# Two layers of attention and FFN on one core: late statistics and output weights split around the first iteration, chunk 7's contexts divided first at chunk 8, last sums closed and normalised one by one

## The chip, the cores and the metric

One core of one Trainium2 chip. The metric is the device time of one execution in microseconds, lower is better. The kernel is a single launch on this core. TensorE is PE in the rows, VectorE is DVE, ScalarE is ACT, GpSimd is POOL, and SyncE's queue is SPq.

## The reference

An array x of 1024 tokens by 512 passes through four steps. Each adds the result of a block to x and normalises the sum over the 512 columns:

```
x = layernorm(x + attn0(x))   # 32 heads of 16; per TOKEN a softmax of q k^T over the heads
x = layernorm(x + ffn0(x))    # three +1/-1 weight matrices, relu between
x = layernorm(x + attn1(x))   # rotary, causal window of 128, 32 query heads and 8 key heads, output weights Wo
x = layernorm(x + moe(x))     # shared experts + the best 2 of 16 experts per token, weighed
```

with `layernorm(x) = (x - mean) / sqrt(var + 1e-5)`. The first attention is unusual: for each token a 32 x 32 matrix of scores between heads, softmax, times the 32 values.

## The kernel before, in words

The tokens are eight tiles of 128 rows (T = 8), kept as X[128, tile, 512] in two groups of four (G = 4). Each engine has its own program, written out by hand in the order in which it is to run; they wait for each other through semaphores. PSUM banks are used in rings: `fill` is PE's wait until a bank is free, `take` the reader's wait until it is full, and `drained` the wait until it has been read.

*First attention.* 16 chunks k, eight for each group, each with the scores of 16 token columns for the four tiles. For a chunk PE makes scores(k + 2), a projection of the other group, and values(k). DVE runs `shift(k + 1)` (maximum and difference, L1010 and L938), `turn_weights(k)` (L1019), and `contexts(k - 1)` (L1025 and L938), which divides the weighted values of the chunk before by their sum. ACT takes the exponentials. At k = NCH = 8 the first group is complete: PE turns its contexts (`contexts(0, ...)`, L424, four banks through a ring of two), which waits for DVE's contexts(7), and DVE adds them to X (`add_contexts`, four additions). Around this POOL and SP issue the small transfers that lay values and keys out for the chunks, and ACT issues loads of later weights.

*Normalisation.* In three steps: DVE's `stats` (L965 and L966: mean and variance of a tile), ACT's `roots` (square root, L1499, where every ACT operation is recorded), DVE's `rates` (L1068, L1069: reciprocal and offset), then ACT's `normalise` for each tile. The semaphores `stats_ready`, `std_ready` and `offset_ready` count batches; the batches are numbered.

*FFN, then second attention.* The second group's last FFN layer (`last_layer(1, j)`) runs inside the loop of the second attention. That loop goes over i = -1 to 7 in eight steps s. In iteration i PE makes the row scores of tile i + 1 (L582), for whose row maxima DVE runs `row_maxima` (L1205), and the key scores of tile i (L595), on which ACT takes exponentials, POOL sets the triangle to zero (L1860, L1863), and PE weighs the values (L610). Row maxima are brought as extra rows into the stack of queries (`turn_maxima`, `maxima_out`, L1219, and POOL's `stack_maxima`, L1852); key scores wait for them. The projections of tile i + 2 (L524), its rotation and its way through DRAM back into stacks (SP L881, POOL L1846) lie in the same iteration; the output of tile i - 1 too. In i = -1 there are no key scores yet. There DVE also sums the FFN result into X (`ffn_out`: L1056, then statistics), takes the rates of batch 4 at step 6, and ACT takes the roots and normalises tiles 4 to 7 at step 6. The output weights `ao` are loaded by SP (L839), copied by ACT (`high_part(15, ...)`, i = 0, step 6) and their rest is subtracted by POOL (L1877, i = 1, step 0).

*MoE and the tail.* Routing, then a list ITEMS of 39: four shared experts for group 0, one for group 1, 31 blocks of 128 routed rows, and the last three shared experts of group 1. For each item PE makes `up(k)`, ACT the silu, DVE the product (for a shared expert with a cast and a difference), and PE `down(k)`. The blocks' results go to DRAM and are gathered again by POOL. For tiles 0 to 3 DVE adds the gathered rows (`combine`). For tiles 4 to 7 PE adds them to the accumulators, through diagonal matrices (`add_routed(t)`, L807), and closes them with the last shared expert (`down`, L761), one flag `sum_closed` for each tile. DVE adds each to X (`collect`), then takes statistics and rates (`last_stats`, batches 7, 8 and 9 for tiles 0 to 3, 4 and 5, 6 and 7), ACT normalises and SP stores (L923).

Of the kernel before, what the change touches and what calls it, by code (L numbers as in the profile page):

```python
# [11 lines left out]
ALU = mybir.AluOpType  # L12
# [6 lines left out]
T = 1024 // P  # L19
G = 4  # L20
# [14 lines left out]
NCH = P // CH  # L35
# [44 lines left out]
def build(nc, x, wq, wk, wv, bias, k0, k1, k2, s0, s1, s2, aq, ak, av, ao, gate, experts, shared,  # L80
          rope_c, factor_c, table_c, out, xs, ys):
    with ExitStack() as ctx:
# [256 lines left out]
        def _(pe):  # L339
# [410 lines left out]
            def down(k):  # L750
                if ITEMS[k][0] == "shared":
# [6 lines left out]
                    for j in range(G):  # L758
                        closed = e == SE - 1
                        for n, (l, r) in enumerate(((hi, dh), (hi, dl), (lo, dh))):  # L760
                            mm = nc.tensor.matmul(acc[j][:, :], l[:, j * P:(j + 1) * P], r,  # L761
                                                  start=(e == 0 and n == 0), stop=(closed and n == 2))
                        if g == 1 and closed:
                            mm.then_inc(sum_closed, 1)
# [45 lines left out]
            for t in range(G, T):  # L810
                add_routed(t)
            down(len(ITEMS) - 1)


# [113 lines left out]
        def _(v):  # L928
# [122 lines left out]
            def ffn_out(g, *which):  # L1051
                ring = (V, A)[g]
                for j in which:
                    t = g * G + j
                    b = ring.take(v, ("ffn", t))
                    nc.vector.scalar_tensor_tensor(X[:, t, :], b[:, :], scales[:, 2:3], X[:, t, :], ALU.mult, ALU.add)\  # L1056
                        .then_inc(ring.free, 1)
                    ring.drained(v, ("ffn", t))
                    ins = stats(t)
                    if j < G - 1 and t > 0:  # L1060
                        ins.then_inc(dve, 1)
                        steps[0] += 1
                    else:
                        ins.then_inc(stats_ready, 1)

# [37 lines left out]
            for k in range(2 * NCH):  # L1103
                if k + 1 < 2 * NCH:
                    shift(k + 1)
# [9 lines left out]
                if k >= 1:  # L1115
                    contexts(k - 1)
# [152 lines left out]
            for i in range(-1, T):  # L1269
                t, r, d = i + 2, i + 1, i - 1  # L1270
                for s in range(8):
# [23 lines left out]
                    if i == -1 and s in (2, 4, 5, 6):  # L1295
                        ffn_out(1, (2, 4, 5, 6).index(s))
                    if s == 5 and r < T:
                        maxima_out(r, 0)
                    if (i, s) == (-1, 6):
                        rates(slice(G, T), 4)  # L1300
# [121 lines left out]
            def last_stats(tiles, batch):  # L1422
# [7 lines left out]
                v.wait_ge(std_ready, batch + 1)  # L1430
                q = slice(tiles[0], tiles[-1] + 1)
                own(nc.vector.reciprocal(rstd[:, q], std[:, q]))
                nc.vector.scalar_tensor_tensor(offset[:, q], mv[:, q, 0], -1.0, rstd[:, q], ALU.mult, ALU.mult).then_inc(offset_ready, 1)

            nshared = 0
            for k, item in enumerate(ITEMS):
# [42 lines left out]
                if k == len(ITEMS) - 2:  # L1479
# [4 lines left out]
                    last_stats(range(0, G), 7)  # L1484

            for a in range(G, T, 2):
                for t in (a, a + 1):
                    v.wait_ge(sum_closed, t - G + 1)
                    collect([t], [banks[4 + t - G]])
                v.wait_ge(x_summed, a + 2)  # L1490
                last_stats(range(a, a + 2), 8 + (a - G) // 2)
# [3 lines left out]
        def _(s):  # L1495
# [190 lines left out]
            for i in range(-1, T):  # L1686
                t, d = i + 2, i - 1
                for step in range(8):
# [15 lines left out]
                    if (i, step) == (-1, 6):  # L1704
                        roots(slice(G, T), 4)
                        s.wait_ge(offset_ready, 5)
                        for t4 in range(G, T):
                            normalise(t4)
                    if (i, step) == (0, 6):
                        high_part(15, 3, raw_c[3], wc_in[3])  # L1710
# [55 lines left out]
            for n, (a, b) in enumerate(((0, G), (G, G + 2), (G + 2, T))):  # L1766
# [7 lines left out]
        def _(p):  # L1774
# [97 lines left out]
            for i in range(-1, T):  # L1872
                t, r = i + 2, i + 1
                for step in range(8):
                    if (i, step) == (1, 0):
# [86 lines left out]
```

## Time and profile before

| | |
|---|---|
| median of 3 runs | 686.64 us (685.29 to 689.45) |
| profiled execution, its own time | 688.42 us |
| its span, first to last instruction | 686.7 us |
| mean granted TensorE clock | 0.952 |
| busy: PE, DVE, ACT, POOL | 596.6, 398.3, 271.0, 221.8 us |
| share of the span | 87%, 58%, 39%, 32% |
| transfers | 99.41 MB, mean 145 GB/s |

The busy time counts an engine's instructions while they run; a matmul's end is modelled. The profile's span is shorter than the time of its execution by what lies around the first and the last instruction. The granted clock is the share of full speed that TensorE was given. In a timeline row the number in brackets is the idle time of that engine before the instruction, and behind the arrow stands what ended it; "issue" is no visible wait, "remote" one whose releaser the profile doesn't tell.

### The profile page before, as it was taken

How to read it: one execution, taken by the hardware profiler on the slowest of the kernel's cores; microseconds unless marked ns; L12 is line 12 of the kernel's file. 1: busy time of each engine (PE TensorE's matmuls, PEld its weight loads, DVE VectorE, ACT ScalarE, POOL GpSimd, SP SyncE). 2: the span in 40 equal slices, each digit the busy share in tenths (PEclk: the TensorE clock that was granted, in tenths of full speed). 3: DMA queues.
4: the chain of work that ended last, by engine and by line, in shares of the span. 5: the costliest groups of instructions: out<-in, count | busy, mean ns of one | idle time of the engine just before them, and what ended most of it. 6: DMA issues, size and time to landing. Idle time of an engine off the chain costs nothing.

```text
span 686.7 us, 13474 instructions
## 1 busy us (share of the span) xinstructions
PE 596.6 (87%) x5125; PEld 470.7 (69%) x5125; DVE 398.3 (58%) x1142; ACT 271.0 (39%) x433; POOL 221.8 (32%) x313
## 2 busy tenths in 40 slices
PE   2998999767898977999999997978799999999894
PEld 1987986656677655776777766755477788788672
DVE  3414643797775767878778787622676243232265
ACT  5155118347744334344353444536410223222205
POOL 5001434264500015544464445451002132231270
PEclk9999999989999988899999999766999999999998
DMA  9100110262134626153361426022115499999373
GB/s 307 68 0 20 48 45 20 63 196 88 40 84 153 215 62 216 42 178 101 118 212 54 171 98 224 4 88 79 50 40 187 156 358 389 389 415 367 118 194 131
DMA packets 45680, 99.41 MB, mean 145 GB/s; under 512 B 11760, under 2 KB 18032, under 8 KB 43440
## 3 DMA queue, kind: packets, MB, share of 16 engines
q1 hardware_dynamic: 27280, 56.70, 22.9%
q0 software_dynamic: 12720, 31.61, 14.6%
q10 hardware_dynamic: 5616, 10.23, 4.1%
q8 instruction: 42, 0.69, 0.4%
q14 instruction: 22, 0.18, 0.1%
HBM read 67.96 MB, written 25.95 MB: 137 GB/s over the span
## 4 chain that ended last, share of the span: by engine, by line
PE 57%; DVE 14%; ACT 11%; DMA 9%; issue 5%; POOL 1%; SPq 1%; ACTq 0%; DVEq 0%
PE bank L343 15%; PE bank L524 11%; PE bank L379 9%; DMA slots_out<-FP 6%; DVE FP L938 5%; ACT FP L1499 4%; PE bank L610 4%; PE bank L595 3%; PE bank L582 3%; PE bank L761 2%; DVE kraw L1205 2%; PE bank L390 2%; ACT W L1499 1%; ACT XR L1499 1%; ACT X L1499 1%
## 5 line engine op out<-in xcount | busy, mean ns | idle before, releaser
L1499 ACT ACTIVATE FP<-bank 128x512 f32<-128x512 f32 (+1 forms) x244 | 138.7, 611 | 289.8 <-PE bank L595 98.8
L1205 DVE CUSTOM_DVE_ANT_0 kraw<-bank,maskb 128x256 bf16<-128x256 f32 (+1 forms) x256 | 88.4, 400 | 33.0 <-PE bank L582 33.0
L524 PE MATMUL bank<-W,XR 128*128 128x512 f32 x348 | 100.6, 432 | 1.6 <-DVE XR L938 1.5
L343 PE MATMUL bank<-FP 128*128 128x128 f32 x558 | 89.0, 312 | 2.4 <-ACT FP L1499 2.4
L379 PE MATMUL bank<-W,XR 128*128 128x512 f32 x288 | 76.2, 414 | 5.2 <-DVE W L938 5.2
L524 PEld LDWEIGHTS bank<-W,XR 128*128 128x128 f32 x348 | 67.0, 204 | 16.4 <-DVE XR L938 2.0
L379 PEld LDWEIGHTS bank<-W,XR 128*128 128x128 f32 x288 | 63.6, 271 | 11.1 <-DVE W L938 5.6
L1894 POOL DMA_INDIRECT FP<-slots_in,index x31 | 29.8, 963 | 125.8 <-PE bank L726 65.8
L1860 POOL TENSOR_SCALAR_AFFINE_SELECT FP<-FP 128x512 f32<-128x512 f32 x64 | 39.7, 644 | 91.6 <-ACT FP L1499 91.6
L343 PEld LDWEIGHTS bank<-FP 128*128 128x128 f32 x558 | 65.6, 192 | 4.9 <-issue 2.9
L938 DVE TENSOR_TENSOR FP<-FP,bank 128x128 f32<-128x128 f32 (+1 forms) x39 | 14.4, 369 | 64.8 <-ACT FP L1499 48.8
L343 PE MATMUL bank<-RP,W 128*128 128x512 f32 x192 | 45.8, 394 | 3.5 <-DVE FP L938 3.5
L1863 POOL TENSOR_SCALAR_AFFINE_SELECT FP<-FP 128x512 f32<-128x512 f32 x56 | 38.9, 719 | 24.2 <-ACT FP L1499 24.2
L343 PEld LDWEIGHTS bank<-RP,W 128*128 128x128 f32 x192 | 35.7, 188 | 12.0 <-issue 1.9
L1820 POOL DMA_DIRECT2D RPF<-FP x64 | 31.7, 502 | 34.8 <-PE bank L415 23.3
L1444 DVE COPY FP<-bank 128x512 f32<-128x512 f32 x31 | 21.4, 691 | 30.0 <-PE bank L726 30.0
L938 DVE TENSOR_TENSOR XR<-bank,XR 128x512 fp32r<-128x512 f32 x27 | 21.3, 805 | 30.2 <-ACT XR L1499 30.2
L610 PE MATMUL bank<-FP 128*17 128x128 f32 x960 | 36.8, 302 | 1.8 <-ACT FP L1499 1.6
L610 PEld LDWEIGHTS bank<-FP 128*17 128x17 f32 x960 | 26.1, 106 | 12.5 <-issue 5.8
L582 PE MATMUL bank<-RP,QS 64*128 64x256 f32 x160 | 21.9, 353 | 11.2 <-DVE hmax L1205 9.6
L595 PE MATMUL bank<-QS,RP 64*128 64x128 f32 x320 | 26.1, 285 | 4.3 <-ACT FP L1499 2.3
L595 PEld LDWEIGHTS bank<-QS,RP 64*128 64x128 f32 x320 | 23.8, 207 | 7.1 <-ACT FP L1499 3.0
(179 smaller groups left out, 960.5 us busy)
## 6 DMA issues: line engine op xcount, KB each, us to landing
FP<-in_experts_dram SPq DMA_DIRECT2D x31, 768.0 KB
slots_out<-QS SPq DMA_DIRECT2D x48, 256.0 KB, 3.0
RP<-slots_out POOLq DMA_DIRECT2D x8, 1024.0 KB, 5.3
slots_out<-FP ACTq DMA_DIRECT2D x31, 256.0 KB
QS<-slots_out POOLq DMA_DIRECT2D x5, 1024.0 KB, 6.8
XR<-slots_out POOLq DMA_DIRECT2D x3, 1024.0 KB, 6.0
FP<-in_shared_dram SPq DMA_DIRECT2D x4, 768.0 KB, 4.3
RPF<-FP POOLq DMA_DIRECT2D x64, 34.0 KB, 2.0
```

Source lines behind the costliest of these rows:

```text
L343: mm = nc.tensor.matmul(bank, lhs, rhs, start=(n == 0), stop=(n == len(terms) - 1))
L379: mm = nc.tensor.matmul(b[:, :], *terms[m], start=(m == 0), stop=(m == 3 * DC - 1))
L524: mm = nc.tensor.matmul(b[:, :], *terms[n], start=(n == 0), stop=(n == len(terms) - 1))
L582: mm = nc.tensor.matmul(both[a][:, m, :], qS[i % 3][half(a, KS), pr, :], kS[half(a, KS), slots, pr, :], start=True, stop=True)
L595: mm = nc.tensor.matmul(both[a][:, m * P:(m + 1) * P], kS[half(a, KS), (i - w) % 4, pr, :], qS[i % 3][half(a, KS), pr, :], start=True, sto ...
L610: mm = nc.tensor.matmul(weighing[32 * q:32 * q + HD + 1, (h // 4 % 4) * P:(h // 4 % 4 + 1) * P], vaug[:, (i - w) % 4, head(h), :], PT[hg % ...
L938: return nc.vector.tensor_tensor(o, a, b, op)
L1205: ins = nc.vector.tensor_tensor_reduce(masked[:, 2 * (f % 2) + m, 0:n], b[:, m, :], maskb[:, m0:m0 + n], 1.0, -BIG, ALU.add, ALU.max, hmax ...
L1499: return nc.scalar.activation(o, i, func, **kw)
L1820: nc.gpsimd.dma_start(vdiag[k % 3][32 * g:32 * g + 32, 272 * g:272 * g + 272].rearrange("p (s d) -> p s d", s=CH), vT[32 * g:32 * g + 32, ...
L1860: ins = nc.gpsimd.affine_select(out=pt, in_=pt, compare_op=ALU.is_ge, fill=0.0, base=0, pattern=[[0, 4], [1, P]], channel_multiplier=-1)
L1863: ins = nc.gpsimd.affine_select(out=pt, in_=pt, compare_op=ALU.is_ge, fill=0.0, base=-1, pattern=[[0, 4], [-1, P]], channel_multiplier=1)
```

## The change

Three parts.

1. At chunk 8 DVE runs contexts(7) ahead of shift(9) and turn_weights(8) instead of behind them.
2. `ffn_out` is cut into `ffn_sum` and `ffn_stats`. In i = -1 the second group's sums stay where they were; all four statistics go to i = 0, step 0, the rates and the roots to i = 0, step 1, and ACT's four normalisations to step 5. ACT's copy of the output weights goes from i = 0, step 6, to i = -1, step 6, and POOL's subtraction from i = 1, step 0, to i = -1, step 7.
3. In the tail `last_stats` no longer takes the rates, so that DVE doesn't wait for the root of tiles 0 to 3 ahead of the last activation. PE adds the routed rows of tiles 4 to 6, closes their sums, and then adds and closes tile 7. DVE takes sums and statistics in turn with the rates; tiles 6 and 7 are normalised as batches of their own.

```diff
@@ tensor
-            def down(k):
+            def down(k, *which):
...
-                    for j in range(G):
+                    for j in which or range(G):
...
-            for t in range(G, T):
+            for t in range(G, T - 1):
                 add_routed(t)
-            down(len(ITEMS) - 1)
+            down(len(ITEMS) - 1, *range(G - 1))
+            add_routed(T - 1)
+            down(len(ITEMS) - 1, G - 1)
@@ vector
+            def ffn_sum(g, j):
+                ring = (V, A)[g]
+                t = g * G + j
+                b = ring.take(v, ("ffn", t))
+                nc.vector.scalar_tensor_tensor(X[:, t, :], b[:, :], scales[:, 2:3], X[:, t, :], ALU.mult, ALU.add)\
+                    .then_inc(ring.free, 1)
+
+            def ffn_stats(g, *which):
...
+            def ffn_out(g, *which):
+                for j in which:
+                    ffn_sum(g, j)
+                    ffn_stats(g, j)
...
             for k in range(2 * NCH):
+                if k == NCH:
+                    contexts(k - 1)
                 if k + 1 < 2 * NCH:
                     shift(k + 1)
...
-                if k >= 1:
+                if k >= 1 and k != NCH:
                     contexts(k - 1)
...
                     if i == -1 and s in (2, 4, 5, 6):
-                        ffn_out(1, (2, 4, 5, 6).index(s))
+                        ffn_sum(1, (2, 4, 5, 6).index(s))
+                    if (i, s) == (0, 0):
+                        ffn_stats(1, *range(G))
...
-                    if (i, s) == (-1, 6):
+                    if (i, s) == (0, 1):
                         rates(slice(G, T), 4)
...
-            def last_stats(tiles, batch):
+            def last_stats(*tiles):
...
                 ins.then_inc(stats_ready, 1)
-                v.wait_ge(std_ready, batch + 1)
-                q = slice(tiles[0], tiles[-1] + 1)
-                own(nc.vector.reciprocal(rstd[:, q], std[:, q]))
-                nc.vector.scalar_tensor_tensor(offset[:, q], mv[:, q, 0], -1.0, rstd[:, q], ALU.mult, ALU.mult).then_inc(offset_ready, 1)
+
+            def last_sum(t):
+
+                v.wait_ge(sum_closed, t - G + 1)
+                collect([t], [banks[4 + t - G]])
...
-                    last_stats(range(0, G), 7)
-
-            for a in range(G, T, 2):
-                for t in (a, a + 1):
-                    v.wait_ge(sum_closed, t - G + 1)
-                    collect([t], [banks[4 + t - G]])
-                v.wait_ge(x_summed, a + 2)
-                last_stats(range(a, a + 2), 8 + (a - G) // 2)
+                    last_stats(*range(0, G))
+
+            rates(slice(0, G), 7)
+            last_sum(G)
+            last_sum(G + 1)
+            v.wait_ge(x_summed, G + 2)
+            last_stats(G, G + 1)
+            last_sum(G + 2)
+            rates(slice(G, G + 2), 8)
+            v.wait_ge(x_summed, G + 3)
+            last_stats(G + 2)
+            last_sum(T - 1)
+            rates(slice(G + 2, G + 3), 9)
+            v.wait_ge(x_summed, T)
+            last_stats(T - 1)
+            rates(slice(T - 1, T), 10)
@@ scalar
                     if (i, step) == (-1, 6):
+                        high_part(15, 3, raw_c[3], wc_in[3])
+                    if (i, step) == (0, 1):
                         roots(slice(G, T), 4)
+                    if (i, step) == (0, 5):
                         s.wait_ge(offset_ready, 5)
                         for t4 in range(G, T):
                             normalise(t4)
-                    if (i, step) == (0, 6):
-                        high_part(15, 3, raw_c[3], wc_in[3])
...
-            for n, (a, b) in enumerate(((0, G), (G, G + 2), (G + 2, T))):
+            for n, (a, b) in enumerate(((0, G), (G, G + 2), (G + 2, T - 1), (T - 1, T))):
                 roots(slice(a, b), 7 + n)
@@ gpsimd
-                    if (i, step) == (1, 0):
+                    if (i, step) == (-1, 7):
                         p.wait_ge(w_high, 16)
                         nc.gpsimd.tensor_tensor(W[:, 7, :], raw_c[3], W[:, 6, :].bitcast(F32), ALU.subtract).then_inc(wo_split, 1)
```

## Rows read from the trace of the kernel before

**Rows 1.** Timeline of chunk 8, all engines: start, us, engine, line, operation, count, idle time.
```profile
133.48 0.68 DVE L1010 TENSOR_REDUCE small<-bank 128x16 f32<-128x512 f32 x1
...
135.43 0.22 DVE L1025 RECIPROCAL small<-bank 128x16 f32<-128x16 f32 x1
...
136.16 3.79 PE L424 MATMUL bank<-ident,FP 128*128 128x128 f32 x16 [3.22 <-DVE FP L938]
137.39 1.47 DVE L938 TENSOR_TENSOR X<-X,bank 128x512 f32<-128x512 f32 x2 [1.28 <-PE bank L424]
...
139.28 1.39 DVE L938 TENSOR_TENSOR X<-X,bank 128x512 f32<-128x512 f32 x2 [0.43 <-PE bank L424]
```

**Rows 2.** Windows, 136 to 140 us: busy time by engine, then clock, DMA share, GB/s.
```profile
136.00:140.00 4.00, 3.84 (x24) 3.20 (x28) 2.18 (x5) 1.44 (x1) 3.91 (x9) 0.57 0.86 262
```

**Rows 3.** Timeline of PE from i = -1 to i = 0.
```profile
244.26 0.44 PE L582 MATMUL bank<-RP,XR 64*128 64x128 f32 x4 [1.50 <-DVE hmax L1205]
247.44 0.80 PE L582 MATMUL bank<-RP,QS 64*128 64x256 f32 x4 [2.75 <-DVE hmax L1205]
...
248.92 4.58 PE L524 MATMUL bank<-W,XR 128*128 128x512 f32 x12
```

**Rows 4.** Timeline of DVE from i = -1 to i = 0.
```profile
243.20 0.27 DVE L1205 CUSTOM_DVE_ANT_0 kraw<-bank,maskb 128x128 bf16<-128x128 f32 x1
...
244.81 0.69 DVE L965 BATCH_NORM_STATS2 st<-X 128x6 f32<-128x512 f32 x1
...
246.08 0.18 DVE L1068 RECIPROCAL rstd<-std 128x4 f32<-128x4 f32 x1 [0.36 <-ACT std L1499]
...
253.96 0.42 DVE L1205 CUSTOM_DVE_ANT_0 kraw<-bank,maskb 128x256 bf16<-128x256 f32 x1 [4.25 <-PE bank L582]
```

**Rows 5.** Timeline of DVE in the tail.
```profile
671.88 0.18 DVE L1432 RECIPROCAL rstd<-std 128x4 f32<-128x4 f32 x1 [4.42 <-ACT std L1499]
...
672.27 0.69 DVE L938 TENSOR_TENSOR FP<-FP,bank 128x512 f32<-128x512 f32 x1
...
675.19 1.37 DVE L938 TENSOR_TENSOR X<-X,bank 128x512 f32<-128x512 f32 x2 [1.05 <-PE bank L761]
```

**Rows 6.** Timeline of ACT in the tail.
```profile
669.64 0.60 ACT L1499 ACTIVATE FP<-bank 128x512 f32<-128x512 f32 x1 [16.19 <-remote]
...
682.71 1.52 ACT L1499 ACTIVATE X<-X,offset,rstd 128x512 f32<-128x512 f32 x2 [0.43 <-DVE offset L1433]
```

**Rows 7.** Timeline of PE in the tail.
```profile
668.22 6.11 PE L807 MATMUL bank<-FP 128*128 128x512 f32 x13 [0.51 <-issue]
674.20 3.00 PE L761 MATMUL bank<-W,XR 128*128 128x512 f32 x12
```

**Rows 8.** Timeline of POOL, then of SP's queue, around i = -1 and 0.
```profile
243.99 1.17 POOL L1852 DMA_DIRECT2D XR<-QS  x2 [8.44 <-DVE QS L1219]
...
272.55 4.54 POOL L1877 TENSOR_TENSOR W<-WF,W 128x2048 fp32r<-128x2048 f32 x1
...
240.74 0.40 SPq L839 DMA_DIRECT2D WF<-in_ao_dram  x1
```

**Rows 9.** Issues of transfers, 238 to 250 us: count, KB each, us to landing.
```profile
WF<-in_ao_dram SPq DMA_DIRECT2D x1, 1024.0 KB, 5.2
XR<-QS POOLq DMA_DIRECT2D x2, 8.0 KB, 2.0
```

**Rows 10.** Timeline of ACT in i = 0.
```profile
249.44 1.28 ACT L1499 ACT_TABLE_LOAD   x1
...
257.84 1.08 ACT L1499 ACTIVATE FP<-bank 128x512 f32<-128x512 f32 x2 [6.03 <-PE bank L595]
...
269.50 1.08 ACT L1499 ACTIVATE FP<-bank 128x512 f32<-128x512 f32 x2 [3.44 <-PE bank L595]
270.48 1.91 ACT L1499 ACTIVATE W<-WF 128x2048 fp32r<-128x2048 f32 x1
```

**Rows 11.** Chain of waits at the end of i = 0: start, us, what.
```profile
268.83 6.82 DMA QS<-slots_out
```

More of the change, by code:

```diff
@@ L1049, in hidden_low @@
                     tt(dst[:, 1, o, :], hf[g][:, o % 2, :], dst[:, 0, o, :].bitcast(F32), ALU.subtract).then_inc(h_ready, 1)
-            def ffn_out(g, *which):
+            def ffn_sum(g, j):
[5 more added lines that the diff above has]
+            def ffn_stats(g, *which):
                 ring = (V, A)[g]
@@ L1054, in ffn_out @@
                     t = g * G + j
-                    b = ring.take(v, ("ffn", t))
-                    nc.vector.scalar_tensor_tensor(X[:, t, :], b[:, :], scales[:, 2:3], X[:, t, :], ALU.mult, ALU.add)\
-                        .then_inc(ring.free, 1)
                     ring.drained(v, ("ffn", t))
```

## The prediction

> **What bounds the kernel now.** I read the page first, then the chain of waits in order of time, to see which engine ends each stage, and then the timelines of the engines at the three places that the change touches. TensorE (PE) holds most of the chain, so an edit pays only where PE, or whoever holds the chain at that moment, waits for the work that is moved. The three places lie one behind the other, and what one gives the next ones pass on: in between, the kernel is chains of waits in a fixed order and loads that start on flags.
>
> **Chunk 8.** VectorE (DVE) works off chunk 9's shift, chunk 8's turned weights and then chunk 7's contexts (reciprocal at 135.43); PE turns the contexts only from 136.16, after 3.22 us of idle time that the difference L938 ends [rows 1]. DVE then waits 1.28 us for the first turned bank and 0.43 us for the third; its four additions end at 140.67 [rows 1]. PE ran these transposes at a mean granted clock of 0.57 over 136 to 140 us [rows 2].
>
> **Around the first iteration (i = -1 and 0).** In i = -1 PE stands 1.50 us before row scores 7 and 2.75 us before the first of i = 0, both times for DVE's maxima [rows 3]. DVE has in between the sum and the statistics of the last FFN tile, a wait of 0.36 us for the root from ScalarE (ACT), and the rates [rows 4]. In i = 0 it is the reverse: PE goes from 248.92 through a product of twelve matmuls in 4.58 us, and DVE stands 4.25 us [rows 3, 4].
>
> **The tail.** DVE waits 4.42 us for the root of tiles 0 to 3 before it touches the last activation [rows 5]; the root stands behind the last silu on ACT, which begins only at 669.64 [rows 6]. PE meanwhile adds the routed rows (thirteen matmuls to 674.33) and then closes four sums [rows 7].
>
> **The change part by part: contexts at chunk 8.** Contexts(7) hold DVE for 0.67 us (135.43 to 136.1) and need nothing but chunk 7's values, which PE had finished before its idle time. Moved to 133.48 they end at 134.15, so that PE may start 2.0 us earlier. The shift and the turned weights (133.48 to 135.43, 1.95 us) follow and end at 136.1; DVE's first addition starts there, 1.28 us earlier. Banks 3 and 4 can be filled only after the first additions. PE's sixteen transposes took 3.79 us, mostly at the lower clock, 0.95 us a bank; at the full level about half. At the full level the additions end near 139.0 (1.7 us gained, both waits); at the lower level each of the last two banks adds up to half a microsecond and they end near 139.7 (1.0 us) [rows 1]. PE's idle time shrinks from 3.22 to about 1.2 us, which speaks for the higher level, yet behind the first two banks PE has little to do. I take 1.3 us. What is late in its place: the shift, by 0.67 us, and with it the exponential and ACT's first conversion of kernel weights. DVE waits for neither in this stretch. If it did, the edit would cost those 0.67 us: the lower bound is a loss of 0.67, the upper a gain of 1.7.
>
> **Statistics and rates out of i = -1.** The last statistics begin at 244.81 and the rates at 246.08, with a reciprocal and a product to 246.4: 1.6 us between the last FFN sum and maxima 7 that go. The statistics of the tile before stand ahead of maxima 6 (243.20), which could start 0.45 us earlier, when its scores are there [rows 4]. So the first row scores of i = 0 start 2.05 us earlier, at 245.4 [rows 3]. Who is late next? The key scores behind them need the first half's maxima: POOL issues those two transfers at 243.99 in 1.17 us [rows 8], and such a transfer lands after 2.0 us [rows 9], near 246.6 if the second starts at 244.6. The maxima leave DVE some 0.6 us earlier, so 246.0, when PE, at 245.4 plus its scores, wants them. That is nearly level and the 2.05 us stand; if the transfer decides, 0.6 us is left.
>
> Four statistics (3.45 us, each 0.69 + 0.17) now stand behind maxima 0 of i = 0. Those end at 249.71 today, so at 247.65; DVE is free at 251.1, 2.85 us before the 253.96 of now [rows 4]. They are hidden in the 4.25 us of idle time, and 2.85 is also the most this part can give. It is reached if PE's product of 4.58 us finds the higher clock, where twelve such matmuls take 3.0 [rows 3, 7]. The rates (0.34 us) go in front of maxima 2 of i = 0; I count 0.1 us for them, since DVE waits a little behind these maxima. I take 2.3 us; bounds 0.6 and 2.85.
>
> **Output weights, roots and normalisation.** The load of the output weights is issued at 240.74 [rows 8] and lands after 5.2 us [rows 9], at 245.9; ACT's copy of 1.91 us [rows 10], now ahead of i = 0, ends at 247.9. Today ACT begins its table load for Exp at 249.44; behind the copy it can begin earlier, and the first exponentials come at 249.2 instead of 250.7. Sqrt now lies between two Exp: two table loads of 1.28 us more, and a root of 0.3 to 0.4. ACT is through with the exponentials at 250.3, has the root behind the statistics (251.1) and its own load (251.6) at 252.0 and the second load at 253.3. The key scores of step 2, at which ACT now stands 6.03 us until 257.84 [rows 10], are due 2.05 to 2.85 us earlier, from 255.0. Hidden. The four normalisations go into step 5: the two of 1.52 us in [rows 6] make 3.0 for four, within the 3.44 us of idle time before 269.50 [rows 10]; their tiles are turned only in iteration 1. POOL's subtraction (4.54 us, today at 272.55 [rows 8]) moves behind the copy, to 247.9; the first mask is kept until 252.4, but the first weighing is some eight microseconds away. That the copy leaves step 6 gives nothing: the next iteration starts on a stack transfer of 6.82 us begun at 268.83 [rows 11], which moves only with the rotation ahead of it.
>
> Here a rule of the Trainium skill speaks against the change. The rows show the table load of 1.28 us begun at 249.44, and nothing but that load in front of the exponential. The page "ScalarE: Activation LUTs" (What ACT_TABLE_LOAD costs) counts about 2.66 us for a switch, since it adds a drain. By that figure, an estimate, the three loads up to step 2 would end some 4 us later than above, 2 us past the need, and the sum would be less by these 2.
>
> **The tail.** Without the wait, the last product, cast and difference (1.9 us, from 672.27 to PE's start at 674.20 [rows 5, 7]) follow the silu's end at 670.25: the activation is there at 672.2. A matmul of the additions costs 0.45 us, a tile 1.8; tiles 4 to 6 are in at 672.5. The first sum reaches DVE 1.0 us later (today 675.19 behind 674.20), at 673.5. From there: two sums 1.4, two statistics 1.7, third sum 0.7, rates 0.35, third statistics 0.85, fourth sum 0.7 (its bank closes near 677.1, as today, for PE's work is only reordered): 679.2. The rates of tile 6 wait for ACT, which normalises 4 and 5 until 679.1 and has the root at 679.4: 679.75; statistics of the last tile 680.6, root 681.0, rates 681.3, one normalisation 0.8: 682.1. Today the last ends at 682.71 + 1.52 = 684.23 [rows 6]. Gain 2.1 us; the store behind it stays. Bounds: 1.6, if the five added hand-overs cost 0.1 us more each, and 2.6, if the first banks close that much earlier. The late silu changes little here: if it came early, the additions would decide in both kernels.
>
> **Sum.** 1.3 + 2.3 + 2.1 = 5.7 us. The profiled execution took 688.42 us (span 686.7 and 1.7 around it), so 682.7 for such a one. It lay 1.8 us above the median of the three runs; against that, 686.64 - 5.7 = 680.9 us.
>
> **Rivals.** (a) Both PE stretches find the higher clock and the banks close early: 1.7 + 2.85 + 2.6 = 7.15, 679.5 us. For it: less idle time of PE. Against: in i = -1 PE still has little to do between 242 and 246. (b) Transfers take most of the first iteration's gain: 1.3 + 0.6 + 2.1 = 4.0, 682.6 us. For it: two arrivals near 246.0. (c) A table load costs ACT twice its 1.28 us when work stands on both sides; three of them make 3.8 us, so ACT is ready at 257.1, 2 us past the need: 5.7 - 2.0 = 3.7, 682.9 us. Against it: the row at 249.44. The page named above holds with this one. (d) Slower: ACT, in program order, stands at the copy until the output weights are there, and all exponentials of i = 0 stand behind it. From the landing to an ACT ready for step 2 are 1.9 + 1.3 + 1.1 + 1.3 + 0.4 + 1.3 = 7.3 us, so 253.2 against 255.0: 1.8 us of slack. Each microsecond beyond costs one; the sum turns negative when the weights land 7.5 us late, a load of 12.7 instead of 5.2 us. At 9 us late: 688 us. No other large load is under way then, so it is unlikely.
>
> **How the numbers follow.** Forecast 0.60, (a) 0.16, (b) 0.13, (c) 0.07, (d) 0.04. A measurement of this kernel can tell about 1% (6.9 us) from no change. The range takes in (a) to (c), both less 1.6 us below and plus 2.1 above, for the lower bound of chunk 8 and the 1.4 us by which the fastest run lay under its median: 677.9 to 685.0. Faster by over 1% means below 679.8: most of (a) and a fourth of the forecast, 0.30. Within 1%: 0.67. Slower: 0.03.
>
> **What would show it.** Right: PE's idle time before the transposes of the contexts near 1 us; no idle time above 2 us on PE around row scores 7 and 0; four statistics in DVE's 4.25 us; two more table loads inside ACT's idle time; the first closed sum 1.7 us ahead of today's, and one normalisation alone at the end. Wrong: row scores of i = 0 early but key scores waiting for a transfer; ACT's copy long in waiting; iteration 1 starting on a transfer that has not moved.

## The result, and the profile after

The changed kernel took 680.81 us (median of 16 runs, 676.62 to 686.01), the kernel before 685.88 us beside it (16 runs, 681.97 to 690.89): ratio 0.9927, 95% interval 0.9903 to 0.9951, so 5.0 us gained. Two later jobs, each with its own runs of the kernel before, gave 0.9914 (0.9879 to 0.9950) and 0.9899 (0.9848 to 0.9951). The profiled execution took 680.29 us, span 678.6, against 688.42 and 686.7. Its mean granted clock is 0.958, before 0.952.

Chunk 8, from the timeline of the changed kernel (columns as in [rows 1]):

```profile
133.41 0.25 DVE L1027 RECIPROCAL small<-bank 128x16 f32<-128x16 f32 x1
...
134.04 0.68 DVE L1012 TENSOR_REDUCE small<-bank 128x16 f32<-128x512 f32 x1
...
135.98 1.25 DVE L940 TENSOR_TENSOR X<-X,bank 128x512 f32<-128x512 f32 x2
137.81 0.69 DVE L940 TENSOR_TENSOR X<-X,bank 128x512 f32<-128x512 f32 x1 [0.57 <-PE bank L424]
138.66 0.69 DVE L940 TENSOR_TENSOR X<-X,bank 128x512 f32<-128x512 f32 x1 [0.17 <-PE bank L424]
139.26 0.68 DVE L1012 TENSOR_REDUCE small<-bank 128x16 f32<-128x512 f32 x1
```
```profile
134.17 1.17 PE L424 MATMUL bank<-ident,FP 128*128 128x128 f32 x8 [1.30 <-DVE FP L940]
136.69 1.93 PE L424 MATMUL bank<-ident,FP 128*128 128x128 f32 x8 [1.35 <-DVE X L940]
```

The contexts' reciprocal is ahead of the shift's reduction, and PE's idle time before the transposes is 1.30 us instead of 3.22 [rows 1]. The first eight transposes take 1.17 us, the last eight 1.93: the granted clock falls to 1.2 GHz at 136.9 us, in between.

Around the first iteration, PE, then DVE, then ACT (against [rows 3, 4, 10]):

```profile
244.37 0.44 PE L582 MATMUL bank<-RP,XR 64*128 64x128 f32 x4 [1.11 <-DVE hmax L1218]
245.90 0.65 PE L582 MATMUL bank<-RP,QS 64*128 64x256 f32 x4 [1.09 <-DVE hmax L1218]
246.40 1.11 PE L595 MATMUL bank<-XR,RP 64*128 64x128 f32 x8
247.45 5.49 PE L524 MATMUL bank<-W,XR 128*128 128x512 f32 x12
...
275.93 0.50 PE L582 MATMUL bank<-RP,QS 64*128 64x256 f32 x4 [2.71 <-DMA QS<-slots_out]
...
277.58 4.24 PE L524 MATMUL bank<-W,XR 128*128 128x512 f32 x12
```
```profile
247.90 0.69 DVE L967 BATCH_NORM_STATS2 st<-X 128x6 f32<-128x512 f32 x1
...
251.01 0.18 DVE L968 BATCH_NORM_AGGREGATE mv<-st 128x2 f32<-128x6 f32 x1
253.42 0.42 DVE L1218 CUSTOM_DVE_ANT_0 kraw<-bank,maskb 128x256 bf16<-128x256 f32 x1 [2.23 <-PE bank L582]
```
```profile
245.97 1.91 ACT L1523 ACTIVATE W<-WF 128x2048 fp32r<-128x2048 f32 x1 [10.43 <-DMA WF<-in_ao_dram]
247.90 1.28 ACT L1523 ACT_TABLE_LOAD   x1
249.19 1.09 ACT L1523 ACTIVATE FP<-bank 128x512 f32<-128x512 f32 x2
250.30 1.28 ACT L1523 ACT_TABLE_LOAD   x1
251.59 0.30 ACT L1523 ACTIVATE std<-mv,epst 128x4 f32<-128x4 f32 x1
251.91 1.28 ACT L1523 ACT_TABLE_LOAD   x1
257.31 1.09 ACT L1523 ACTIVATE FP<-bank 128x512 f32<-128x512 f32 x2 [4.12 <-PE bank L595]
```

PE's two waits are 1.11 and 1.09 us instead of 1.50 and 2.75. Key scores follow at 246.40 without a wait, so no transfer stands in their way. DVE has the four statistics where it stood idle. ACT has three table loads, nothing between a load and its user, and still 4.12 us of idle time. But PE's product takes 5.49 us, which was 4.58 [rows 3], and iteration 1 begins on a stack transfer at 275.93, where it began at 275.75 before. Counted from the first row scores of i = -1 (228.13, before 227.64) that is 47.8 us for 48.1: in this profile the 2.0 us are down to 0.3 there.

The tail, in the same order (against [rows 5 to 7]):

```profile
661.59 5.31 PE L807 MATMUL bank<-FP 128*128 128x512 f32 x12
666.34 2.65 PE L761 MATMUL bank<-W,XR 128*128 128x512 f32 x9
668.83 1.88 PE L807 MATMUL bank<-FP 128*128 128x512 f32 x4
670.14 1.26 PE L761 MATMUL bank<-W,XR 128*128 128x512 f32 x3
```
```profile
664.59 0.17 DVE L1079 RECIPROCAL rstd<-std 128x4 f32<-128x4 f32 x1
...
667.64 1.38 DVE L940 TENSOR_TENSOR X<-X,bank 128x512 f32<-128x512 f32 x2 [2.69 <-PE bank L761]
```
```profile
656.34 0.60 ACT L1523 ACTIVATE FP<-bank 128x512 f32<-128x512 f32 x1 [7.56 <-PE bank L343]
...
671.64 1.52 ACT L1523 ACTIVATE X<-X,offset,rstd 128x512 f32<-128x512 f32 x2 [0.55 <-DVE offset L1080]
...
675.30 0.81 ACT L1523 ACTIVATE X<-X,offset,rstd 128x512 f32<-128x512 f32 x1 [0.43 <-DVE offset L1080]
```

The rates of tiles 0 to 3 cost no wait, sums 4 to 6 close before the last tile is added, and one normalisation of 0.81 us ends it at 676.11. From the first addition to that end it is 14.53 us, where it was 17.98 (684.23 less the first of the sixteen additions, of which [rows 7] has the last thirteen):

```profile
666.25 1.45 PE L807 MATMUL bank<-FP 128*128 128x512 f32 x3
```

The last silu came at 656.34, after 7.56 us of idle time: the 16.19 us of [rows 6] are in none of the other profiles.

### The profile page after: what moved, and what is told of

It is laid out like the page before. It is cut to its first block, busy times and chain, and to the rows that moved or that the text cites. A ratio compares the mean times of both kernels' runs of the same rounds, so it can differ in the third digit from the quotient of the medians.

```text
span 678.6 us, 13479 instructions
## 1 busy us (share of the span) xinstructions
PE 595.0 (88%) x5125; PEld 469.4 (69%) x5125; DVE 397.3 (59%) x1144; ACT 274.0 (40%) x436; POOL 221.3 (33%) x313
## 4 chain that ended last, share of the span: by engine, by line
PE 62%; DVE 12%; ACT 10%; DMA 8%; issue 5%; POOL 1%; SPq 1%; DVEq 0%; ACTq 0%
PE bank L343 19%; PE bank L524 11%; PE bank L379 9%; DVE FP L940 5%; ACT FP L1523 4%; DMA slots_out<-FP 4%; PE bank L610 4%; PE bank L582 3%; PE bank L595 3%; PE bank L761 2%; PE bank L402 2%; PE bank L390 2%; PE bank L726 1%; DVE kraw L1218 1%; ACT XR L1523 1%
## 5 line engine op out<-in xcount | busy, mean ns | idle before, releaser
L940 DVE TENSOR_TENSOR FP<-FP,bank 128x128 f32<-128x128 f32 (+1 forms) x39 | 14.4, 369 | 63.3 <-ACT FP L1523 47.5
L343 PE MATMUL bank<-RP,W 128*128 128x512 f32 x192 | 45.8, 394 | 3.5 <-DVE FP L940 3.5
L1845 POOL DMA_DIRECT2D RPF<-FP x64 | 31.6, 501 | 34.1 <-PE bank L415 23.0
L582 PEld LDWEIGHTS bank<-RP,QS 64*128 64x128 f32 x160 | 13.1, 195 | 22.4 <-DVE hmax L1218 11.1
```

Of the source, the lines that this page charges most:

```text
L343: mm = nc.tensor.matmul(bank, lhs, rhs, start=(n == 0), stop=(n == len(terms) - 1))
L582: mm = nc.tensor.matmul(both[a][:, m, :], qS[i % 3][half(a, KS), pr, :], kS[half(a, KS), slots, pr, :], start=True, stop=True)
L940: return nc.vector.tensor_tensor(o, a, b, op)
L1845: nc.gpsimd.dma_start(vdiag[k % 3][32 * g:32 * g + 32, 272 * g:272 * g + 272].rearrange("p (s d) -> p s d", s=CH), vT[32 * g:32 * g + 32, ...
```

## The experiments

Twelve experiments: nine new kernels, and three times one that had run before. Each has 6 to 12 runs, against 23 or 35 runs of the kernel before in the same job, and one profile. The gains in microseconds are worked out from the ratio. The time says what all of a kernel did; beside it I read three stretches of each profile, since the middle, which no edit touches (from the row scores of i = 6 to the first addition of the tail), took anything from 241.8 us (the first profile of the change) to 249.1. In the second and third profile of the change it took 246.1 and 243.4, in the kernel before 246.5, so most of what made the first one's middle short was chance.

**Each part alone, and the whole again.** Chunk 8's order only:

```
+                if k == NCH:
+                    contexts(k - 1)
...
+                if k >= 1 and k != NCH:
```

> Only chunk 7's contexts go ahead at chunk 8. If the parts add up (theory A), the additions at chunk 8 end 1.3 us earlier and the time is 1.3 us (0.2%) under before. If PE's clock level or a transfer takes the gain back before the second attention starts (theory B), the additions end 1.3 us earlier all the same, the first row scores of i = -1 start within 0.5 us of before, and the time is before's within 1 us.

The statistics, roots, rates, normalisations and output weights only:

```
+                        ffn_sum(1, (2, 4, 5, 6).index(s))
+                    if (i, s) == (0, 0):
+                        ffn_stats(1, *range(G))
...
+                        high_part(15, 3, raw_c[3], wc_in[3])
```

> Only the statistics, rates, roots, normalisations and output weights move around the first iteration. Theory A: first row scores of i = 0 2 us earlier, row scores of i = 1 2.3 us earlier, time 2.3 us under before. Theory B: the first is 2 us earlier, but PE's product behind it takes 5 us or more at the lower clock and the stack transfer 7 us or more, so the row scores of i = 1 start at most 0.5 us earlier and the time is before's within 1 us.

The tail only, both PE's order and the sums one by one:

```
+            down(len(ITEMS) - 1, *range(G - 1))
+            add_routed(T - 1)
...
+            last_sum(G + 2)
+            rates(slice(G, G + 2), 8)
```

> Only the tail is changed. Theory A: from the first addition of routed rows to the last normalisation 2.1 us less than in before's profile (18.0 us), time 2.1 us under before. Theory B (the tail is nearly all of the change): 3 us or more less, and the time 3.5 to 5 us under before.

All three, unchanged:

> The changed kernel once more, for a second profile and as the measure of the other three. Both theories: 4 to 6 us under before. If the 4.8 us by which the stretch from the second iteration to the first addition was shorter in its first profile were chance, it is another number here; if it belongs to the change, 4 us or more again.

Measured, against a before of 688.92 us: chunk 8 ratio 0.9983 (0.9945 to 1.0020), -1.2 us; first iteration 0.9972 (0.9928 to 1.0016), -1.9 us; tail 0.9969 (0.9930 to 1.0008), -2.1 us; all three 0.9914 (0.9879 to 0.9950), -5.9 us. (The plain medians, 686.67, 686.46, 685.75 and 680.93 us, lie 2.3, 2.5, 3.2 and 8.0 us under it.) The parts add up to -5.2, and nothing speaks for a part that works only beside another, within intervals that are some 5 us wide. None of the three alone is told from zero by its interval; the profiles have to do that:

| stretch | profiles without the part | with it | gain |
|---|---|---|---|
| chunk 8: copy of its values to the shift of chunk 10 | 8.99 to 9.51 (7) | 8.25 to 8.29 (4) | 0.7 to 1.3 |
| the same copy to the first row scores | 96.55 to 97.57, mean 97.16 (7) | 96.25 to 97.11, mean 96.62 (4) | 0.5 |
| row scores of i = -1 to those of i = 0 | 19.80 to 19.83 (6) | 17.76 to 17.77 (4) | 2.05 |
| row scores of i = -1 to those of i = 6 | 191.5 to 194.3, mean 192.8 (5) | 190.0 to 191.7, mean 190.6 (4) | 2.2 |
| first addition to the end of the last normalisation | 16.81 to 18.04, mean 17.4 (5) | 14.52 to 14.53 (4) | 2.9 |

So, by the means, the first iteration keeps what it gains, chunk 8 has lost half of it by the first row scores, and the tail gives more than its share. In the second and fourth row the ranges overlap, so that half is not told from nothing or from all. A fifth profile with the new order at chunk 8, that with the first iteration filled (below), has the same program up to 228 us: it was granted the full clock over 134 to 140 us and took 7.61 us for the first stretch, and still 96.57 us for the second.

The theories: by the first row scores chunk 8 alone is within 0.5 us of before (96.2 us for 96.6), as its theory B has it, but its time, 1.2 us under, is theory A's, and the interval holds both. In the profile of the first iteration's edits alone the row scores of i = 1 come 45.8 us behind those of i = -1, where it was 48.1: theory A. In the three profiles of the whole change it is 47.8, 46.9 and 47.5. PE's product took 4.61 us there and 5.49, 4.18 and 5.49 in those three (4.5 to 5.0 in the five without the part), the stack transfer 6.9 to 8.0 us (6.4 to 7.0): theory B's slow product and transfer come in some executions, and the gain at i = 1 moves with them between 2.3 and 0.3 us. The tail alone is 3.5 us shorter than in the first profile of the kernel before, as in its theory B, with the time of theory A.

**Why the old tail is 16.8 us in two profiles and 17.4 to 18.0 in three.** In the three PE stops within its sixteen additions. With the first iteration's edits alone it waits for the gathered rows of the last tile:

```profile
666.35 5.31 PE L807 MATMUL bank<-FP 128*128 128x512 f32 x12
672.63 1.98 PE L807 MATMUL bank<-FP 128*128 128x512 f32 x4 [0.96 <-DMA FP<-slots_out,slots]
```

In the profile of 17.42 us the same wait is 0.34 us, and in the kernel before the sixteen additions take 8.08 us instead of 7.03, with 0.51 us of idle time whose releaser the profile doesn't name [rows 7]. Two of the three have their last silu in time, so the silu is not what makes a tail long. In all seven profiles with the new tail it takes 14.52 or 14.53 us. The last tile's additions start there 7.24 us behind the first addition (668.83 - 661.59), and in the profile above, wait included, 6.28 us behind it: PE's new order leaves room for late rows. How often they are late is not known from five profiles.

**The tail taken apart.** Both kernels are the kernel before with one side of the tail's edit, and nothing at chunk 8 or in the first iteration. First the one-by-one side without PE's order; against the kernel with the whole tail's edit:

```
-            down(len(ITEMS) - 1, *range(G - 1))
-            add_routed(T - 1)
-            down(len(ITEMS) - 1, G - 1)
+            down(len(ITEMS) - 1)
```

> Only the tail's sums, rates and normalisations one by one (vector and scalar engine), with TensorE's order of the last weighings and divisions left as before. Theory 1 (the gain is that the last normalisations no longer wait for the joint rates): the stretch from the last chunk's first divided product to the last normalisation's end is 14.5 us as with the whole tail edit. Theory 2 (TensorE's order gives a part): 15.5 to 16.5 us, between 14.5 and the 18.0 of before. Time: 2 us under before by theory 1, 1 to 1.5 us under by theory 2.

Then PE's order without the one-by-one side; against the same:

```
-            last_sum(G + 2)
-            rates(slice(G, G + 2), 8)
...
+            for a in range(G, T, 2):
...
+                last_stats(range(a, a + 2), 8 + (a - G) // 2)
```

> Only TensorE's order at the end is the changed one (the last expert's products for three tiles ahead of the last tile's weighing); sums, rates and normalisations stay in pairs. The tail ran 16.8 us in most profiles of kernels with the old tail (18.0 with a stall), 16.4 us with the one-by-one side alone, 14.5 us with both. Theory 1 (the two sides add up): TensorE's order gives the 1.9 us that the other side lacked, the tail is 14.9 to 15.3 us. Theory 2 (either side needs the other): with the sums in pairs the first pair still closes as late as before for VectorE, and the tail is 16 us or more. Time: 1.5 to 2 us under before by theory 1, within 0.8 by theory 2.

Measured: the one-by-one side alone 1.0017 (0.9991 to 1.0044), +1.2 us; PE's order alone 0.9962 (0.9932 to 0.9992), -2.6 us. The timelines of PE and of DVE tell why. One by one, PE's order as before:

```profile
669.19 7.19 PE L807 MATMUL bank<-FP 128*128 128x512 f32 x16
675.82 3.30 PE L761 MATMUL bank<-W,XR 128*128 128x512 f32 x12
```
```profile
677.12 1.37 DVE L938 TENSOR_TENSOR X<-X,bank 128x512 f32<-128x512 f32 x2 [4.56 <-PE bank L761]
```

PE's order, in pairs:

```profile
667.59 5.31 PE L807 MATMUL bank<-FP 128*128 128x512 f32 x12
672.34 2.65 PE L761 MATMUL bank<-W,XR 128*128 128x512 f32 x9
```
```profile
673.64 1.38 DVE L940 TENSOR_TENSOR X<-X,bank 128x512 f32<-128x512 f32 x2 [2.15 <-PE bank L761]
...
677.40 1.27 DVE L940 TENSOR_TENSOR X<-X,bank 128x512 f32<-128x512 f32 x2
```

DVE's first sum starts 7.93 us behind the first addition in one (677.12 - 669.19) and 6.05 in the other. From the first addition to the end the tail is 16.39 us in one, 15.10 in the other, 14.53 with both, and 16.81 in the profiles of the old tail that have no stall. So PE's order is worth 1.7 us alone and the one-by-one side 0.4 alone and 0.6 behind it: theory 2 of the first experiment and theory 1 of the second. Cut at the first sum the sides add exactly: up to it 6.05 us with PE's order, alone or with both (7.76 without it and without a stall), and from it to the end 8.47 and 8.48 us one by one, 9.04 and 9.05 in pairs. The 0.4 is 0.6 less 0.17 us, by which the additions were slower in that one profile (7.19 for 7.03). The time of the one-by-one side alone is no gain where 1 to 1.5 us were expected; its interval, from a gain of 0.6 us to a loss of 3.0, just holds what its profile shows.

**The first iteration taken apart.** The statistics, roots, rates and normalisations moved, the weights' copy and subtraction left at (0, 6) and (1, 0), and nothing at chunk 8 or in the tail; against the kernel with all of the first iteration's edits:

```
                     if (i, step) == (-1, 6):
-                        high_part(15, 3, raw_c[3], wc_in[3])
...
+                    if (i, step) == (0, 6):
+                        high_part(15, 3, raw_c[3], wc_in[3])
```

> Of the first iteration's edits only the statistics, roots, rates and normalisations are moved; the output weights' last high part stays at (0, 6) and GpSimd's subtraction at (1, 0). Theory 1 (the statistics alone held the maxima): the stretch from the first row scores of iteration -1 to those of iteration 0 is 17.8 us as with all these edits (19.8 before), and the time is 1.5 to 2.5 us under before. Theory 2 (the weights' move carries a part, by the subtraction off GpSimd's row in iteration 1): the stretch is 17.8 us but iteration 1 is longer than the 30.5 to 31.1 us with the edits by 0.5 us or more.

Measured: 0.9967 (0.9938 to 0.9996), -2.3 us; i = -1 takes 17.8 us, so the statistics alone give it. i = 0 takes 30.0 us (28.0 to 30.0 in four profiles with the weights moved too), i = 1 31.5. PE now waits for ACT before a weighing, since the copy of 1.91 us stands ahead of what PE needs from it:

```profile
274.55 1.91 PE L610 MATMUL bank<-FP 128*17 128x128 f32 x32 [1.80 <-ACT FP L1510]
```
```profile
272.00 1.91 ACT L1510 ACTIVATE W<-WF 128x2048 fp32r<-128x2048 f32 x1
```

It takes the place of the wait for the stack transfer, so i = 0 is no longer for it. Iteration 1 is 0.4 to 2.0 us longer than with the move (29.5 to 31.1 in four profiles), theory 2 in its sign, and from the row scores of i = -1 to those of i = 6 it is 192.4 us, 0.7 to 2.4 more than in those four. Against it: with the weights in their old place and the old statistics, iteration 1 took 29.5 to 29.6 us in four profiles and 31.9 in a fifth, so one profile of 31.5 can be chance. The times (-2.3 and, with the weights, -1.9) do not separate the two. What the weights' move gives is not settled.

**Is the clock what holds the rest?** In the changed kernel PE is granted 1.2 GHz from 246.1 us for 6.8 us. The waits just before it are those of 1.11 and 1.09 us above. Idle stretches were filled with transposes of the identity that nobody reads: six each before row scores 7 of i = -1 and the first of i = 0, eight and two in i = 0, fourteen at its end:

```
+                    if (i, s) in ((-1, 6), (-1, 7)):
+                        warm(weighing, 6)
+                    if (i, s) in ((0, 4), (0, 5)):
+                        R.drained(pe, ("qkv", 2, 2))
+                        warm(banks[6], (8, 2)[s - 4])
...
+                if i == 0:
+                    warm(banks[6], 14)
```

> The whole change, with idle stretches of TensorE around the first iteration filled by transposes of the identity whose results nobody reads. Theory A (the clock that TensorE is granted takes the gain back): the product after iteration -1's key scores takes 3.0 to 3.5 us instead of 5.5, the long products behind the stack's wait in iteration 1 take about 3.75 us instead of 4.2 to 4.6, iterations 0 and 1 together are 2 to 3 us shorter than with the change alone (59.6 to 61.1 us), and the time is 1.5 to 3 us under that of the change. Theory B (the stack's transfer sets when iteration 1 begins, whatever the clock): the row scores of iteration 1 start as with the change, about 1.8 to 2 us behind iteration 0's own work, and the time is that of the change within 0.7 us.

And chunk 8 too:

```
+                    A.drained(pe, ("heads", 1, 2, HD // 4 - 1))
+                    warm(banks[2], 6)
+                    contexts(0, 0, 1)
+                    warm(banks[2], 7)
+                    contexts(0, 2, 3)
...
+                if k in (10, 11):
+                    warm(banks[2], 14)
```

> The same with further transposes of the identity around chunk 8's first contexts and ahead of the values of chunks 10 and 11. Theory A: the transposes of the low attention matrix behind chunk 8, 1.97 us in the change's profile, take 1.3 to 1.4 us, and the stretch from the copy of chunk 8's values to the first row scores is 1 us shorter than the change's 96.5 to 97.1 us; the time is 0.5 to 1 us under the kernel with the first iteration filled alone. Theory B: that stretch stays at 96.3 to 97.1 us, for its waits are on VectorE and transfers, and the time is as with the first iteration filled alone, or up to 1 us longer by the transposes themselves.

And the first set of transposes in the kernel before:

> The kernel before with the first iteration's filling transposes. Theory A: if the clock alone is what the gain hangs on, before gains too, 1 to 2 us, in iterations 0 and 1 (28.3 and 29.7 us before). Theory B: nothing, or up to 0.6 us more by the transposes themselves.

Last, the change and the version with both fillings in one job:

> The changed kernel again, to stand beside the next one on the same chip: 0.990 to 0.994 of before.

> The changed kernel with both fillings again. Theory A (the clock's half level takes a part of the gain, and the fillings win it back): 2 to 4 us under the changed kernel of the same job, mean granted clock of its runs above 0.965 where the change's are at 0.96. Theory B (the difference between the jobs was chance): within 1 us of it.

Measured: first iteration filled 0.9885 (0.9848 to 0.9921), 680.41 us; both filled 0.9862 (0.9826 to 0.9898), 678.28 us; kernel before, filled, 0.9978 (0.9944 to 1.0012), 687.12 us. In the last job the change alone took 680.55 us, 0.9899 (0.9848 to 0.9951; 0.990 to 0.994 expected), and with both fillings 677.69 us, 0.9837 (0.9792 to 0.9882). The mean granted clock over the runs of each was 0.953 (before), 0.958 and 0.960 (the change), 0.960 (before, filled), 0.968 (first filled), 0.972 and 0.973 (both). PE with both fillings, in the timeline:

```profile
245.19 3.03 PE L534 MATMUL bank<-W,XR 128*128 128x512 f32 x12
...
271.47 0.51 PE L592 MATMUL bank<-RP,QS 64*128 64x256 f32 x4 [1.83 <-DMA QS<-slots_out]
...
272.76 3.01 PE L534 MATMUL bank<-W,XR 128*128 128x512 f32 x12
```

And windows of the changed kernel, then of the one with both fillings (columns as in [rows 2]):

```profile
146.00:156.00 10.00, 6.71 (x183) 5.49 (x172) 9.00 (x21) 8.67 (x12) 5.16 (x11) 0.83 0.51 148
244.00:256.00 12.00, 10.54 (x44) 7.95 (x45) 9.22 (x42) 7.15 (x7) 6.82 (x5) 0.72 0.13 44
...
266.00:280.00 14.00, 10.86 (x95) 8.25 (x96) 7.75 (x39) 6.08 (x11) 5.00 (x9) 0.64 0.53 171
```
```profile
146.00:156.00 10.00, 8.21 (x209) 6.41 (x197) 9.73 (x22) 9.51 (x13) 5.88 (x12) 1.00 0.55 158
244.00:256.00 12.00, 10.52 (x66) 7.87 (x67) 11.49 (x45) 8.84 (x10) 8.10 (x7) 1.00 0.03 7
...
266.00:280.00 14.00, 11.77 (x109) 9.50 (x109) 8.41 (x39) 4.01 (x8) 4.64 (x8) 1.00 0.31 107
```

The same product takes 3.03 us (3.02 in the second profile with both fillings), where it was 4.18 to 5.49 in the three profiles of the change, and that behind the stack 3.01 for 4.24 (4.39 in that second profile, in which the clock fell once more behind the stack's wait). From row scores -1 to those of i = 6 it is 186.3 and 187.8 us in the two profiles with both fillings (mean 190.6 in the four without), and from chunk 8's copy to the first row scores 94.7 and 95.8 us (mean 96.6). The stack transfer still ends last before iteration 1, with 1.83 us of waiting: theory B has the wait right, but the transfer is issued when the rotated rows are there, and that comes with the clock (at 264.5 and 265.0 us, in three profiles of the change at 266.1 to 268.3). So theory A stands for the two fillings together: 2.9 us under the change in the job that ran both, where the slowest of six runs with the fillings (678.67 us) is faster than the fastest of six without (678.74). The first job with both fillings had no run of the change; its 678.28 us lie 2.3 to 2.7 us under the change's three medians in other jobs, and 2.1 us under the first filling alone beside it, where 0.5 to 1 was expected.

With the first iteration alone filled it is not shown. The product there took 4.61 us where 3.0 to 3.5 was expected, since the clock fell at 247.3 all the same; i = 0 and 1 took 58.4 us (59.3 to 61.1 in the change), 0.8 to 2.6 us less where 2 to 3 was expected, but i = -1 to 6 took 191.7, and the time is that of the change within its interval. The lower level itself became rarer: up to 300 us it was granted for 23.9 to 30.7 us in the three profiles of the change (23.9 to 34.1 in all ten without fillings), for 13.7 us here, and for none and 6.8 us with both fillings. In the kernel before, the same transposes gave -1.5 us with an interval that holds zero, and in its profile the clock fell for 6.8 us at 248.6. Why transposes 100 us earlier make the difference at 246 us is open.

## Why the prediction was right

680.9 us was forecast, 680.81 came; against the kernels before beside it, 5.7 forecast, 5.0, 5.9 and 6.9 measured. The likeliest case came by its own steps. That the medians agree to 0.1 us is luck: the kernel before had 686.64 us in the forecast and 685.88 beside the change, and of the terms chunk 8's came out smaller and the tail's larger than forecast.

- **Contexts at chunk 8: 1.3 us forecast, about 1.0 at the next shift (mean against mean), 0.5 by the first row scores.** The contexts end 0.04 us off (134.11 for 134.15), the first addition comes at 135.98 for 136.1, PE's idle time is 1.30 us for 1.2. The bank waits (0.57 and 0.17 us) lie between those of the two levels, as the mean between the bounds assumed; at the full level, in the fifth profile, only 0.21 us is left. Not weighed: that behind the stretch the clock is at the lower level again for a part (0.83 over 146 to 156 us, as before the change), and that, by the means, half a microsecond of the gain does not reach the first row scores. With both places filled that longer stretch is 0.8 to 1.9 us shorter.
- **First iteration: 2.3 forecast, 2.0 on the spot and 2.2 by i = 6.** The 2.05 us are there to a few hundredths. "Nearly level" for the transfer of the maxima was right, and (b) fell: key scores wait for nothing. The 0.25 us on top, from a product at the higher clock, did not come: the product took 5.49, 4.18 and 5.49 us, no shorter than before on the mean. One of the forecast's own signs of being wrong did appear: in the first profile iteration 1 starts on a stack transfer that has hardly moved (0.3 us), with a product 0.9 us longer and a transfer 0.7 us longer (7.55 for 6.82). In the other two profiles it has moved by 0.6 and 1.3 us, and by i = 6 the mean of the gain is 2.2, with ranges that touch. The forecast had named the transfer and gave it no price of its own.
- **Output weights: hidden, as costed.** The copy ended its wait at 245.97 (245.9 forecast), the first exponentials came at 249.19 (249.2), ACT was through at 253.2 (253.3) and then stood 4.12 us, more than the 1.8 us of slack worked out, because PE's product was long. (d) had no occasion.
- **Table loads.** (c) is refuted by the rows: three loads of 1.28 us, the root 0.01 us behind its load and the second 0.02 us behind the root. The 2.66 us of the Trainium skill ("ScalarE: Activation LUTs", What ACT_TABLE_LOAD costs) would give 8.0 us for the three (an estimate); the stretch from 247.90 to 253.19 holds them, two exponentials and a root in 5.3 us, and the trace decides.
- **Tail: 2.1 forecast, 2.3 against old tails without a stall (16.81), 2.9 against the mean of the five, 3.45 against the very profile that the sum was worked out from.** The last two are above the bound of 2.6: the forecast took over the additions of a profile in which they had been held up by 1.05 us (8.08 for 7.03), as if the changed kernel would have the same. The step that the path led with, the wait for the root behind a late silu, was an accident of the profiled execution: the idle time of 16.19 us is in no other one. The prediction said that with an early silu the additions would decide in both kernels, and so it was, by PE's order with 1.7 us (the sign named in advance, the first closed sum 1.7 us ahead: 6.05 us behind the first addition for 7.76); the sums one by one give the other 0.6.
- **The sum.** 0.5 + 2.2 + 2.9 = 5.6 us by the means of the profiles, 5.2 by the parts measured alone. With scatter of about 1 us in each stretch, both agree with 5.7 and with the 5.0 to 6.9 of the three jobs. The 1.6 and 2.1 us by which the forecast widened its range are not worked out from rows.

## What to carry to other kernels

Where one engine waits in a fixed order for a step whose result is needed only later, move the step into that engine's next idle stretch, and check every engine that the moved result passes; the 2.05 us worked out so came as 2.0. At a closing chain, first reorder the producer so that its partial results close before its last long input, and only then split the consumer. And read the granted clock where time has been freed: shorter waits did not raise it in the first iteration, and filling idle stretches of TensorE in two places gave another 2.9 us, beside the 5 to 7 of the change. And before a term is taken from one profile, look at a second: here the same unedited tail took 16.8 to 18.0 us.

## What the runs showed of the hardware

- **Clock and scatter.** Over 35 executions of the kernel before, time and mean granted clock go together, which of them leads was not tested (correlation -0.80, 6.1 us for each 0.01 of clock; 12 runs of the change: -0.71 and 4.7 us). In the other two jobs it is -0.64 and -0.75 over 23 executions each, and in one kernel, the tail's one-by-one side alone, +0.10 over 12. A good part of the scatter between executions of one kernel (682.8 to 694.8 us there) goes along with it, but not always.
- **A half level behind short waits.** In the profile of the change the clock fell to 1.2 GHz at 246.1 us behind waits of PE of 1.11 and 1.09 us, between single groups of 0.44 and 0.65 us of work; a product of 2.12 us ended at 242.78. In the three profiles of the change and the one with the first iteration filled it fell at 245.6 to 247.3 us; with both fillings not at all in this stretch.
- **The last silu's releaser.** The wait named "remote" (16.19 us, [rows 6]) appeared in one profile of fourteen; in the other thirteen it is 7.56 us, for PE's bank. In that profile it did not decide: the last activation was there at 674.14, PE's additions ended at 674.33. One profile of a kernel is not enough to tell a wait from an accident.
